# Edge MLP of a graph network: the attributes' product takes a row of ones and the bias, and relu becomes one instruction

## The reference

```python
ei = jnp.concatenate([x[src], edge_attr], axis=-1)        # 256 + 64 features of an edge
core = jnp.maximum(ei @ W1 + b1, 0.0) @ W2 + b2
gate = jax.nn.sigmoid(ei @ Wg + bg)
msg = gate * core
agg = jax.ops.segment_sum(msg, dst, num_segments=x.shape[0])
out = agg + x                                             # then a layer norm with gamma, beta
```

## Time and profile before

| | us |
|---|---|
| median of 3 runs | 3920.31 |
| the runs | 3916.71, 3920.31, 3924.02 |
| span of the profiled execution, first to last instruction | 3924.5 |
| PE busy over the span | 3261.1 (83%) |
| DVE busy | 2815.4 (72%) |
| POOL busy | 2087.1 (53%) |
| ACT busy | 1882.4 (48%) |

### The profile page before, as it was taken

One profiled execution on the slowest core, in us unless ns is written; L12 is line 12 of the kernel. 1 busy time (PEld: TensorE's weight loads), 2 busy tenths in 40 slices (PEclk: granted clock), 3 DMA queues, 4 the chain that ended last, 5 costly groups with the idle time before them and its releaser, 6 DMA issues. The chain is left out here.

```text
span 3924.5 us, 56642 instructions
## 1 busy us (share of the span) xinstructions
PE 3261.1 (83%) x14868; PEld 2626.7 (67%) x14868; DVE 2815.4 (72%) x7890; ACT 1882.4 (48%) x5403; POOL 2087.1 (53%) x2120
## 2 busy tenths in 40 slices
PE   5999927688576899477999993599999999999865
PEld 4888715476454566245777772587878787888754
DVE  5676768698587466794666662598989898989733
ACT  3777705466333121142333331366666666666555
POOL 4767500475365666033333322476767676767667
PEclk8999958899799999657999996799999999999998
DMA  5788739443375333183333335886868686878765
GB/s 145 244 244 247 235 95 354 153 134 108 107 211 174 94 88 87 54 247 99 111 116 115 111 110 187 283 252 199 251 201 252 197 251 201 253 208 242 209 210 164
DMA packets 690467, 710.71 MB, mean 181 GB/s; under 512 B 73444, under 2 KB 644190, under 8 KB 689796
## 3 DMA queue, kind: packets, MB, share of 16 engines
q1 hardware_dynamic: 592204, 484.13, 39.8%
q0 software_dynamic: 68288, 181.26, 17.1%
q10 hardware_dynamic: 29660, 41.70, 3.2%
HBM read 427.77 MB, written 296.22 MB: 184 GB/s over the span
## 5 line engine op out<-in xcount | busy, mean ns | idle before, releaser
L616 POOL DMA_INDIRECT s_i_messages<-h,table_row x600 | 614.0, 1023 | 190.4 <-issue 158.3
L2801 PE MATMUL s_i_bank<-s_i_messages,s_i_equal 128*128 128x256 f32 x1200 | 362.5, 386 | 74.3 <-issue 36.6
L926 POOL TENSOR_TENSOR n_powers<-n_powers,neg_half 128x8 f32<-128x8 f32 (+3 forms) x164 | 268.5, 1637 | 229.9 <-DVE n_powers L891 149.4
L851 ACT ACTIVATE n_z<-gamma_bc,n_powers 128x256 f32<-128x256 f32 x320 | 174.8, 593 | 356.5 <-POOL n_powers L926 356.5
L810 PE MATMUL s_n_bank<-w,n_xt 128*128 128x256 f32 x1280 | 306.9, 383 | 22.6 <-DMA n_xt<-in_x_t 22.6
L828 PE MATMUL s_n_bank<-w_out,n_ht 128*128 128x256 f32 x1280 | 311.7, 387 | 5.6 <-ACT n_ht L838 5.3
L2838 DVE SCALAR_TENSOR_TENSOR s_i_y<-s_i_bank,s_i_scale,s_i_acc 128x256 f32<-128x256 f32 x600 | 285.2, 476 | 34.3 <-PE s_i_bank L2801 32.2
L819 PE MATMUL s_n_bank<-n_x3t,w_in 128*128 128x256 f32 x1280 | 303.2, 380 | 0.0
L2801 PEld LDWEIGHTS s_i_bank<-s_i_messages,s_i_equal 128*128 128x128 f32 x1200 | 219.3, 193 | 101.1 <-issue 42.2
L810 PEld LDWEIGHTS s_n_bank<-w,n_xt 128*128 128x128 f32 x1280 | 246.0, 192 | 58.0 <-DMA n_xt<-in_x_t 23.8
L828 PEld LDWEIGHTS s_n_bank<-w_out,n_ht 128*128 128x128 f32 x1280 | 247.3, 195 | 46.2 <-ACT n_ht L838 11.9
(11 more groups left out here) (444 smaller groups left out, 9169.7 us busy)
## 6 DMA issues: line engine op xcount, KB each, us to landing
h<-s_i_y SPq DMA_DIRECT2D x600, 128.0 KB, 3.9
n_xt<-in_x_t SPq DMA_DIRECT2D x160, 256.0 KB
out<-n_w SPq DMA_DIRECT2D x160, 256.0 KB
s_i_equal<-eq_tab SPq DMA_DIRECT2D x600, 64.0 KB
x<-s_x_rows SPq DMA_DIRECT2D x100, 256.0 KB
out<-s_a_hs SPq DMA_DIRECT2D x100, 128.0 KB
proj_dst<-s_a_hd SPq DMA_DIRECT2D x100, 128.0 KB
h<-s_h_rows SPq DMA_DIRECT2D x50, 256.0 KB, 4.1
```

The source lines that it names most:

```text
L616: return net.nc.gpsimd.indirect_dma_start(out, None, table, bass.IndirectOffsetOnAxis(index, 0))
L851: sc = self.nc.scalar.activation(self.Z[u][:, g, :], self.net.bc["gamma"][:], ACT.Identity, bias=v[:, 8 + g:9 + g], scale=v[:, 10 + g:11 + g])
L926: self.nc.gpsimd.tensor_tensor(v[:, 8 + b0:8 + b1], v[:, b0:b1], self.net.neg_half[:, 0:b1 - b0], ALU.pow).then_inc(self.powered, 1)
L2801: nc.tensor.matmul(banks[r % 4][:, 0:D], EQ[q % NM][:], M[q % NM][:], start=True, stop=True).then_inc(summed, 1)
```

## The change

The weights of the attributes get a 65th row that holds the bias `bm1`. The hidden layer's product takes all 65 rows of the attribute tile, the row of ones too, and PE's wait for the ones stands ahead of `hidden` instead of `gate`. The relu has no bias any more and covers both halves in one instruction. The column of `bm1` is no longer kept, and the load of a row of 256 numbers into `w_m1e` takes the place of the load of 128x2 numbers as columns.

```diff
-        self.col_names = ["b1", "bm1", "b_in"]
-        self.cols = sb("cols", [P, 3, C])
+        self.col_names = ["b1", "b_in"]
+        self.cols = sb("cols", [P, 2, C])
...
-        self.w_m1e = sb("w_m1e", [self.DE, D])
+        self.w_m1e = sb("w_m1e", [self.DE + 1, D])
...
-            (net.w_m1[:], chunks(a["wm1"][0:D, :])), (net.w_m1e[:], a["wm1"][D:D + net.DE, :]),
+            (net.w_m1[:], chunks(a["wm1"][0:D, :])), (net.w_m1e[0:net.DE, :], a["wm1"][D:D + net.DE, :]),
+            (net.w_m1e[net.DE:net.DE + 1, :], a["bm1"].unsqueeze(0)),
...
                     past(pe, relu_ready, k)
+                    pe.wait_ge(ones_ready, NB)
                     for m in range(C):
                         out = hds[:, m * G * P:(m + 1) * G * P]
                         for c in range(C):
                             nc.tensor.matmul(out, net.w_m1[:, c, m * P:(m + 1) * P], xt[:, c, :], start=c == 0, stop=False)
-                        mm = nc.tensor.matmul(out, net.w_m1e[:, m * P:(m + 1) * P], at[0:DE, :], start=False, stop=True)
+                        mm = nc.tensor.matmul(out, net.w_m1e[:, m * P:(m + 1) * P], at[:, :], start=False, stop=True)
...
                     past(pe, tanh_ready, k)
-                    pe.wait_ge(ones_ready, NB)
...
-                    for m in range(C):
-                        mv = nc.scalar.activation(RL[:, m, :], hds[:, m * G * P:(m + 1) * G * P], ACT.Relu, bias=net.cols[:, 1, m:m + 1])
-                    mv.then_inc(relu_ready, 1)
+                    nc.scalar.activation(RL[:].rearrange("p c e -> p (c e)"), hds[:, :], ACT.Relu).then_inc(relu_ready, 1)
```

More of the change, by code:

```diff
@@ L351, in _ @@
         def _(sp):
-            with nc.allow_non_contiguous_dma("three biases as columns, once"):
+            with nc.allow_non_contiguous_dma("two biases as columns, once"):
                 for dst, src in keys:
@@ L837, in silu @@
         for m in range(self.C):
-            mv = self.nc.scalar.activation(self.HT[:, m, :], self.hd[:, 2 * m * P:2 * (m + 1) * P], ACT.Silu, bias=self.net.cols[:, 2, m:m + 1])
+            mv = self.nc.scalar.activation(self.HT[:, m, :], self.hd[:, 2 * m * P:2 * (m + 1) * P], ACT.Silu, bias=self.net.cols[:, 1, m:m + 1])
         mv.then_inc(self.ht_ready, 1)
```

## The result

| | before | changed |
|---|---|---|
| median, us | 3919.91 (4 runs) | 3876.76 (4 runs) |
| lowest and highest | 3916.71, 3924.02 | 3875.76, 3881.72 |
| ratio | | 0.9892, 95% interval 0.9878 to 0.9906 |
| span of the profiled execution | 3924.5 | 3874.0 |
| that execution's own time | | 3875.76 |

The change is worth 43 us, or 1.1%; the forecast was 3880.6 with a range of 3871 to 3891. In the changed kernel the profiled execution's own time is 1.8 us above its span. If the same lies around the first span, the profiled execution of before took about 3926.3 us, 6 more than its median, so that the difference of the two spans, 50.5 us, is more than the change made.

The account below looks back on a forecast made before the run. PE alone was taken to bound the edge MLP. Pauses of 38.7 us plus 1.0 in turn 0 gave 39.7 us off the 3924.5 us span, 3884.8, and 4.2 less for the median: 3880.6 us, range 3871 to 3891.

Parts of the forecast that it names:

- main term: Edge MLP: the attribute product over 65 rows removes four pauses, 0.79 us a turn, 38.7 us over 49 turns.
- the loads' reading: Upper bound from starts of weight loads in hidden layer and gate: 0.89 us a turn, 45 us in all.
- the four idle times of 0.33 us: Widest bound: all idle time ahead of weight loads at the borders goes, 1.3 us a turn or 66 us.
- Turn 0: MLP's first turn, PE at half clock: 1.17 us computed, 1.0 taken, if the clock rises at the same moment.
- Relu, bias, moved wait, loads at the start: Remaining parts of the change, all costed at zero; ScalarE saves about 0.25 us a turn that nobody waits for.
- What is late next: After the MLP's turn shrinks to 10.37 us, VectorE's wait becomes 2.9 us and ScalarE keeps 1.1 us worst-turn slack.
- The offset to the median: Whole kernel: the profiled span, 3924.5 us, lies 4.2 us above the median; the forecast carries the same offset.
- Nothing is given back: Denies the rival that h's store lands later and PE waits for the relu: 10 us, time 3891; chance 5%.
- The pause hid no more than the starts showed: Denies the rival that pauses in the MLP cost up to 66 us, time 3855; chance 4%.
- That the row count isn't the cause: Rival: the hidden layer's pause comes from w_m1e's weights or accumulation and stays, time 3920; chance 5%.
- Slower by the clock: Rival: PE without pauses is granted less clock; a tenth of the stage at half clock gives 3932; chance 2%.

Follow-up runs that it names:

- eight borders: Kernel before with the gate's product of the attributes over 64 rows too, leaving out the gate's bias; 3954.72 us, ratio 1.0093.
- second pair of profiles: Kernel before and changed kernel, both unaltered, each profiled a second time; one execution each, 3912.24 us and 3881.89 us.
- The relu alone: Kernel before with only the relu made one instruction of 128x512, leaving out the bias bm1; 3918.92 us, ratio 1.0004.
- the run with the zero row: Kernel before with the hidden layer's attribute product over 65 rows, the 65th weight row zero, bias still in the relu; 3877.27 us, ratio 0.9892.
- the run with the products side by side: Kernel before with the second half's hidden products reordered so the two 64-row products are adjacent; 3902.85 us, ratio 0.9957.

## Why the prediction was right

**The bound.** PE alone sets the MLP's pace. The runs bear it out from both sides: eight borders or none move the time by what they cost PE, and ScalarE can do four more relus a turn while PE waits for it in only a few turns.

**The size of the main term.** The forecast took 0.79 us a turn from the starts of matmuls; 0.78 was measured. Of the bounds, the loads' reading (0.89) and the four idle times of 0.33 us (1.3) were too large. The idle time of the loads isn't what the border costs. Elsewhere the loads run one matmul ahead: in the earlier trace rows the first load of L2472 starts at 2115.48 and its matmul at 2115.70. At a border load and matmul start together, at 2112.41 and 2112.42. What PE loses there shows in the starts around it (timeline of PE in short windows, which show single matmuls, kernel before):

```profile
2112.11 0.38 PE L2459 MATMUL s_g_bank<-s_g_xt,w_m 128*128 128x256 f32 x1
...
2112.74 0.38 PE L2460 MATMUL s_g_bank<-s_g_attr,w_m1e 64*128 64x256 f32 x1
2113.04 0.48 PE L2459 MATMUL s_g_bank<-s_g_xt,w_m 128*128 128x256 f32 x1
```

The first has 128 rows; the next, of 64, starts at 2112.42, 0.31 us behind it instead of 0.216, and the one behind that at 2112.74, 0.32 us later. The next border, to 2113.04, begins the same way, and the matmul there is longer, 0.48 us instead of 0.38. Twice 0.1 us too much is the 0.195 of a border. It is about the 0.22 us by which a load leads elsewhere, and not the whole 0.33 for which it sits idle. Distances between starts of the bounding engine give the price, idle times of its helper don't.

**Turn 0** is the one term with a premise that failed. I took 1.0 us; in the first pair of profiles it gave 3.7 (11.42 to 7.68), since the clock rose ahead of the gate and not behind it (timeline of PE, changed kernel):

```profile
1804.89 1.91 PE L2461 MATMUL s_g_bank<-s_g_xt,w_m 128*128 128x256 f32 x4
...
1809.97 1.03 PE L2472 MATMUL s_g_bank<-w_g,s_g_xt 128*128 128x256 f32 x4
...
1812.57 1.89 PE L2484 MATMUL s_g_bank<-w_m,s_g_relu 128*128 128x256 f32 x8
```

12 instructions take 5.08 us up to 1809.97, and the next 12 take 2.60. The sum with the measured terms is 49 x 0.78 + 3.7 = 41.9, and the MLP shrank by 41.8. The assumption that failed is that the clock rises at the same moment again. In the second pair of profiles turn 0 gave 0.7 (6.86 to 6.16) and the MLP shrank by 40.2. So the 3.7 belong to two executions and not to the change, and that 1.0 lies between the two is luck.

**Relu, bias, moved wait, loads at the start.** All were costed at nothing. The relu alone moves nothing, and the 65 rows without the bias in them give the whole gain. The wait for the ones shows nowhere among PE's waits. The wait for the loads at the start ended 0.18 us earlier.

**What is late next.** VectorE's wait went to 2.9 us a turn, as worked out. ScalarE's worst slack was put at 1.1 us and is 1.6 in the profile, as the longest wait for the store was 6.6 us in it and not 7.1.

**The offset to the median.** The sum was made against the span and carried over by 4.2 us. The forecast is 3.8 us above the measured median, within the 6 us between the changed kernel's own runs. The forecast gain of 39.7 us lies inside the interval of the measured one, 37 to 48, and the run with the zero row, in another group, gained 40. What the 3.8 us consist of can't be told: turn 0 of a single profile doesn't speak for a median.

**The rivals.** Nothing is given back: silu waits for the store of h in 14 of 43 turns, where it was 12 of 45, but the list of waits has no PE waiting for a relu. The pause hid no more than the starts showed, 5.19 us for the 24 instructions where 5.18 were forecast. That the row count isn't the cause fell with the zero row. The Trainium skill's sentence on it (*TensorE: Matmul & The Clock Gate*, Step-by-step: what each phase is for) holds for the load itself: two loads of 64 rows take 0.40 us where the row count doesn't change ahead of them (L2460 of the run with the products side by side), two of 65 rows 0.41. That sentence says nothing of what happens between products of different row counts. The Trainium skill's page *TensorEngine Tiling (Array Packing)*, Key Properties, does: a change of tiling mode drains the engine. The runs agree with it in that each change between 128 or 65 rows and 64 or 32 costs time, 0.195 us; that it is a drain which takes this time no trace shows. Slower by the clock: 1.00 was granted from 1830 to 2300 us, where the prediction had asked for it, and 504 matmuls started in 100 us:

```profile
core 0: us, PE busy (x) PEld busy (x) DVE busy (x) ACT busy (x) POOL busy (x), PEclk, DMA share, GB/s
1830.00:2300.00 470.00, 470.00 (x2358) 415.06 (x2357) 328.53 (x910) 174.18 (x318) 169.62 (x226) 1.00 0.40 121
```

## What to carry to other kernels

A product over 64 or 32 rows that stands between products of 128 rows costs a pause at both sides, here 0.195 us each at full clock (float32, 128x256). A 65th row (a bias with a row of ones, or zeros) takes both pauses away; if it can't be had, put such products side by side. Other row counts, and 32 rows beside 64, were not run. A PE that is "busy" for the whole stretch can still lose 7% of a turn in this way: count its matmuls in a stretch, or the distance of their starts, and look for "issue" ahead of its weight loads.

## What the runs showed that was not expected

**The clock at the stage's start.** With the twelve later ones there are fourteen profiles, and each gives the time from the first hidden product to the second layer's. Of the seven with four or eight borders a turn, four are long (11.42, 11.43, 11.43, 11.02 us) and three short (6.86, 7.98, 7.79). The other seven, with two borders or none, are all short (6.2 to 7.7 us). All run at half clock first and at full clock later; only the moment of the rise differs, by some us, between executions of the unchanged kernel too. Whether the pauses make a late rise likelier stays open: four of seven against none of seven points that way, and a second profile of the same kernel went the other way. It is worth about 4 us once in an execution, not in every turn.

**The bias operand of ScalarE.** Before, each relu of 128x256 with a column of biases took 474 ns; in the run with two relus and no bias the same shape took 384, and the single one of 128x512 takes 597. The run with the zero row, which has a bias and no pauses of PE, has 473. So reading a bias from a column costs 90 ns an instruction here. The Trainium skill (*ScalarE: Activation LUTs*, What ACT_TABLE_LOAD costs) gives about 93 ns for such an operand, and the trace agrees.

```profile
L2559 ACT ACTIVATE s_g_relu<-s_g_bank x100: 377/384/396, 1815.3 to 2319.1; 128x256 f32<-128x256 f32 x100
```
